# Pacing 313 gathers by an event each, with at most two gathers in flight

## The chip, the core and the metric

The kernel runs on one core of a Trainium2 chip, which has a matrix engine (TensorE, PE in the profile), a vector engine (VectorE, DVE), a scalar engine (ScalarE, ACT), GpSimd (POOL) and a queue engine (SyncE, SP), each with an instruction stream of its own. The streams meet in semaphores only. The metric is the device time of one launch in microseconds; lower is better.

## The reference

The function scores 2048 samples of 26 categorical fields. Each field of a sample picks one row of a table with 12500 rows; a row holds 16 embedding numbers and one first-order weight.

```
emb  = embed_table[f, x_idx]                       # (N, 26, 16)
lin1 = w1_table[f, x_idx].sum(1) + w1_bias
fm   = 0.5 * ((emb.sum(1) ** 2).sum(-1) - (emb * emb).sum((1, 2)))
mlp  = relu(relu(emb.reshape(N, 416) @ W1 + b1) @ W2 + b2) @ W3 + b3
last = x0 = emb.transpose(0, 2, 1)
for W in (cin_w0, cin_w1, cin_w2):                 # CIN layers
    last = einsum('ndl,ndf,klf->ndk', last, x0, W); feats.append(last)
out  = lin1 + fm + mlp + concat(feats).sum(1) @ lin_w + lin_b
```

## The kernel before

The CIN sum over its output channels lets the weights be folded into small matrices first; that is the setup, on PE, DVE and ACT, with its weights loaded by SP's and ACT's DMA queues. The samples then come in T = 16 tiles of 128. In each tile the embeddings lie in `emb` (three buffers, tile t in buffer t % 3), 128 partitions by 26 fields by 17 numbers.

*Where the rows come from.* POOL issues one indirect DMA, a gather, for each field of a tile (line 500): 128 rows of 68 bytes, one a partition. Tiles 0 and 1 gather all 26 fields. From tile 2 on the last four fields are not gathered: PE and DVE look them up in tables that are held in SBUF (`look_rows`, `keys_to_one_hot`, `pick_row`). So there are 2 * 26 + 14 * 22 = 360 gathers, numbered 0 to 359 below; gather 52 is the first of tile 2. Every gather adds 16 to its tile's semaphore `gathered[t]` when it has landed.

*What a tile does.* Its work is cut into 14 units: two halves in which the transposed embeddings are made (`x_high`, `x_low`), and NU = 12 units of the pairwise products (`square` on ACT, `z_low` on DVE, `main` and `picked` on PE). ACT ends its part of a unit by raising `hi_ready`, DVE by raising `lo_ready`, so both count units, 14 a tile; `x_no(t, h)` and `s_no(t, u)` give the number of a unit. PE, DVE and ACT pass units to one another through a ring of three PSUM banks.

*Who waits for the gathers.* ACT's `copy_by_position(t)` (lines 564 to 569) reorders tile t's embeddings into `by_pos`. It runs at unit u = 10 of tile t-1, waits for all of tile t's gathers and for its four looked-up fields, and stands in ACT's stream ahead of `square(t-1, 10)`. For the last tile the copy is cut in two (`copy_last_early`, `copy_last_late`) after u = 11. PE's `x_half` waits for the copy. In the setup the first copy, `copy_by_position(0)` at line 674, stands in ACT's stream ahead of six DMAs that move blocks of the setup (lines 676 to 682).

*What paces POOL* (lines 484 to 502). Before the gathers with the positions 16, 22, 34, 41 and 47 POOL waits for an event of the setup. Tile t >= 3 needs its buffer free: `by_pos_ready` and `row_sums` of tile t-3. From tile 2 on every second gather also waits for a unit of tile t-3 in `hi_ready`. Any number of gathers may be in flight.

Of the kernel before, what the change touches and what calls it, by code (L numbers as in the profile page):

```python
# [32 lines left out]
LOOKS = 4  # L33
FIRST_LOOK = 2
LATER = 2
EARLY = 18
PER_UNIT = 2
COLS = 98
WIDE = 26
SHARES = 4  # L40
# [57 lines left out]
def deepfm_cin_kernel(nc, x_idx, rows, w1_bias, mlp_w1, mlp_b1, mlp_w2, mlp_b2, mlp_w3, mlp_b3,  # L98
                      cin_w0, cin_w1, cin_w2, lin_w, lin_b, out):
    N, F = x_idx.shape  # L100
# [5 lines left out]
    T = N // P  # L106
# [13 lines left out]
    NC = 3  # L120
# [4 lines left out]
    NX = 2  # L125
    NPROD = NX + NU
# [14 lines left out]
    with ExitStack() as ctx:  # L141
# [6 lines left out]
        def sem(name):  # L148
            return ctx.enter_context(nc.semaphore(name))
# [19 lines left out]
        EMB = 3  # L169
# [132 lines left out]
        m_done, m_copied, b_done, b_copied = sem("m_done"), sem("m_copied"), sem("b_done"), sem("b_copied")  # L302
        ap_ready, bp_ready = sem("ap_ready"), sem("bp_ready")
        t_copied = sem("t_copied")
        y_blocks, yl_block, s_blocks = sem("y_blocks"), sem("yl_block"), sem("s_blocks")
        y_copied, y_stored = sem("y_copied"), [sem(f"y_stored{n}") for n in range(7)]
        moved_in, t_in = [sem(f"moved_in{g}") for g in range(3)], sem("t_in")
        t_step, total_ready = sem("t_step"), sem("total_ready")
        by_row_done, by_row_copied = sem("by_row_done"), sem("by_row_copied")
        za_done, zlin_done = sem("za_done"), sem("zlin_done")  # L310
# [10 lines left out]
        keys_first_in, keys_in = sem("keys_first_in"), [sem(f"keys_in{b}") for b in range(2)]  # L321
        one_hot_ready, rows_out = sem("one_hot_ready"), sem("rows_out")
        look_masked, looked = sem("look_masked"), sem("looked")
        gathered = [sem(f"gathered{t}") for t in range(T)]
        gathered_late = sem("gathered_late")
        by_pos_ready = sem("by_pos_ready")
        filled = sem("filled")
        hi_ready = sem("hi_ready")
        lo_ready = sem("lo_ready")
# [18 lines left out]
        def s_no(t, u):  # L348
            return NPROD * t + NX + u

        def looks(t):

            return LOOKS if FIRST_LOOK <= t < T else 0

        def look_no(t, i):
            return LOOKS * (t - FIRST_LOOK) + i

        def look_at(t, slot):

            n = LOOKS * t + slot - LATER  # L360
            return (FIRST_LOOK + n // LOOKS, n % LOOKS) if 0 <= n < look_no(T, 0) else None

        def looked_by(t):

            return min(max(LOOKS * t + 1 - LATER, 0), look_no(T, 0))
# [117 lines left out]
        @block.gpsimd  # L483
        def _(pool):
            pool.iota(row_base[:], pattern=[[V, F]], base=0, channel_multiplier=0).then_inc(base_ready, 1)
            SETUP_STEPS = {16: (m_done, 1), 22: (b_done, 1), 34: (s_blocks, 1), 41: (by_row_done, 1), 47: (za_done, 1)}
            for t in range(T):
                if t < 2:
                    pool.wait_ge(ix_ready, t + 1)
                if t >= EMB:  # L490
                    pool.wait_ge(by_pos_ready, 2 * (t - EMB + 1))
                    pool.wait_ge(row_sums, t - EMB + 1)
                for f in range(F - looks(t)):
                    if F * t + f in SETUP_STEPS:
                        signal, value = SETUP_STEPS[F * t + f]
                        pool.wait_ge(signal, value)
                    if t >= EMB - 1 and f and f % PER_UNIT == 0:
                        behind = s_no(t - EMB, NC + f // PER_UNIT - 1) if t >= EMB else s_no(0, f // PER_UNIT)
                        pool.wait_ge(hi_ready, behind + 1)
                    pool.indirect_dma_start(emb[t % EMB][:, f, :], None, rows,  # L500
                                            bass.IndirectOffsetOnAxis(row_ix[:, t, f:f + 1], 0)
                                            ).then_inc(gathered[t] if t < T - 1 or f < EARLY else gathered_late, 16)

        def within(mat, g, width):

# [14 lines left out]
        def _(act):  # L520
# [29 lines left out]
                               accum_out=first[:, t:t + 1]).then_inc(row_sums, 1)  # L550

            def copy_last_early():
                act.wait_ge(gathered[T - 1], 16 * EARLY)
                act.wait_ge(looked, look_no(T - 1, LOOKS))
                for fs in (slice(0, EARLY), slice(F - LOOKS, F)):
                    act.activation(by_pos[:, :, fs], emb[(T - 1) % EMB][:, fs, 0:D].rearrange("p f d -> p d f"), ACT.Copy)

            def copy_last_late():
                fs = slice(EARLY, F - LOOKS)
                act.wait_ge(gathered_late, 16 * (F - LOOKS - EARLY))  # L560
                act.activation(by_pos[:, :, fs], emb[(T - 1) % EMB][:, fs, 0:D].rearrange("p f d -> p d f"),
                               ACT.Copy).then_inc(by_pos_ready, 2)

            def copy_by_position(t):
                act.wait_ge(gathered[t], 16 * (F - looks(t)))
                if looks(t):
                    act.wait_ge(looked, look_no(t, LOOKS))
                act.activation(by_pos[:], emb[t % EMB][:, :, 0:D].rearrange("p f d -> p d f"),
                               ACT.Copy).then_inc(by_pos_ready, 2)
# [54 lines left out]
            def tile(t):  # L624
                for u in range(NC, NU):
                    if u == NU - 2 and t + 1 < T - 1:
                        copy_by_position(t + 1)
                    square(t, u)
                    if u == NU - 1 and t + 1 == T - 1:
                        copy_last_early()  # L630
                        copy_last_late()
                    if t == 0 and u in LOOK_SPLIT:
                        look_high(LOOK_SPLIT[u])
                    if t == 0 and u == 8:
                        second_high()
                    if u == 5:
                        hidden1(t)
                    if u == 7:
                        hidden1_high(t)
# [32 lines left out]
            act.wait_ge(keys_out, 1)  # L672
            act.activation(key_t[:], ps_s[0][0:T * LOOKS, 0:P], ACT.Copy).then_inc(keys_copied, 1)
            copy_by_position(0)
            act.wait_ge(moved_zeroed, 1)
            move(act, 3)
# [629 lines left out]
```

## Time and profile before

| | us |
|---|---|
| time, median of 3 runs | 512.74 (511.46 to 513.53) |
| profiled execution, first to last instruction | 694.2 |
| PE busy | 510.3 |
| DVE busy | 412.8 |
| ACT busy | 389.0 |
| POOL busy | 356.6 |
| mean granted TensorE clock | 0.863 |

The profiled execution is a different one from the timed runs. Its span is the only time that it has; of what lies around the span nothing is recorded. The page gives busy time by engine, the chain of work that ended last, and groups of like instructions with their mean and with the idle time before them. The windows view gives the same for chosen stretches.

### The profile page before, as it was taken

The page shows a single profiled execution, that of the slowest core. Times are in us where ns is not written, and L with a number is a line of the kernel's source. Part 1 is how long each engine was busy: PE and PEld are TensorE (multiplying, and loading weights), DVE is VectorE, ACT ScalarE, POOL GpSimd, SP SyncE. Part 2 cuts the span into 40 slices and gives each one's busy share as a digit, 9 for nine tenths or more (in the row PEclk, how much of TensorE's full clock was granted, in tenths as well). Part 3 has the DMA queues.
Part 4 walks back from the last instruction along what each step waited for, and adds up shares of the span by engine and source line. Part 5 has one row for each costly group of instructions (what it writes and reads, how often), then busy time and mean ns, then how long its engine had stood idle before and what let it go on. Part 6 is the DMA issues. An engine that isn't in the chain of part 4 may idle for free.

```text
span 694.2 us, 6825 instructions
## 1 busy us (share of the span) xinstructions
PE 510.3 (74%) x2235; PEld 415.1 (60%) x2235; DVE 412.8 (59%) x680; ACT 389.0 (56%) x759; POOL 356.6 (51%) x365
## 2 busy tenths in 40 slices
PE   2897918824696959588695959596886949599988
PEld 2865705723484838476574747475765737478666
DVE  6431227903475748376584847484765848478866
ACT  0321628604464847376574847484665748378875
POOL 6665666774465464637466454547374664510000
PEclk9995666975896979979798989899797979899999
DMA  8836434221111111202111111112021111100000
GB/s 176 163 21 117 88 62 103 7 7 5 5 6 7 4 6 4 7 4 8 5 6 5 5 6 6 6 4 8 3 9 5 6 5 5 6 3 1 0 1 0
DMA packets 21508, 15.57 MB, mean 22 GB/s; under 512 B 12790, under 2 KB 19811, under 8 KB 21347
## 3 DMA queue, kind: packets, MB, share of 16 engines
q0 software_dynamic: 11520, 3.16, 13.5%
q1 hardware_dynamic: 6949, 9.99, 5.9%
q10 hardware_dynamic: 3005, 2.01, 1.4%
q8 instruction: 18, 0.29, 0.2%
q14 instruction: 16, 0.12, 0.1%
HBM read 14.92 MB, written 0.21 MB: 22 GB/s over the span
## 4 chain that ended last, share of the span: by engine, by line
PE 28%; DVE 24%; another core or an unknown queue 18%; ACT 15%; issue 11%; DMA 3%; SPq 0%; DVEq 0%
DVE z_lo L803 5%; ACT ps_s L598 5%; ACT z_hi L591 4%; PE ps_y L1197 4%; PE ps_y L1198 3%; DVE ps_y L946 3%; DVE one_hot L935 3%; PE ps_s L1097 2%; DMA w_space<-cin_w 2%; DVE sums L829 2%; PE ps_q L1111 2%; ACT room_a L597 2%; DVE ps_q L814 2%; DVE emb L950 2%
## 5 line engine op out<-in xcount | busy, mean ns | idle before, releaser
L500 POOL DMA_INDIRECT emb<-rows,idx_raw x360 | 356.3, 990 | 253.7 <-issue 101.4
L803 DVE TENSOR_TENSOR z_lo<-ps_s,z_hi 128x512 fp32r<-128x512 f32 (+1 forms) x192 | 132.1, 688 | 138.9 <-ACT ps_s L598 87.6
L591 ACT ACTIVATE z_hi<-ps_s 128x512 fp32r<-128x512 f32 (+1 forms) x192 | 114.2, 595 | 171.9 <-remote 105.6
L1197 PE MATMUL ps_y<-look_hi,one_hot 128*128 128x442 f32 x224 | 92.6, 413 | 91.4 <-DVE one_hot L935 89.6
L598 ACT ACTIVATE ps_s<-ps_s 128x512 f32<-128x512 f32 (+1 forms) x192 | 113.5, 591 | 0.7
L1111 PE MATMUL ps_q<-z_lo,zw_hi 128*127 128x512 f32 (+1 forms) x192 | 86.9, 453 | 32.6 <-DVE z_lo L803 21.1
L1197 PEld LDWEIGHTS ps_y<-look_hi,one_hot 128*128 128x128 f32 x224 | 49.5, 221 | 101.0 <-DVE emb L950 57.1
L1198 PE MATMUL ps_y<-look_lo,one_hot 128*128 128x442 f32 x224 | 89.3, 400 | 0.0
L946 DVE SCALAR_TENSOR_TENSOR ps_y<-tables,look_place,ps_y 128x442 f32<-128x442 f32 x56 | 37.9, 677 | 78.6 <-remote 70.6
L1097 PE MATMUL ps_s<-xt,pick 128*128 128x512 f32 (+1 forms) x192 | 77.1, 414 | 8.6 <-ACT x L582 5.4
L1113 PE MATMUL ps_q<-z_hi,zw_hi 128*127 128x512 f32 (+1 forms) x192 | 78.9, 411 | 0.0
L1112 PE MATMUL ps_q<-z_hi,zw_lo 128*127 128x512 f32 (+1 forms) x192 | 78.9, 411 | 0.0
L1111 PEld LDWEIGHTS ps_q<-z_lo,zw_hi 128*127 128x127 f32 (+1 forms) x192 | 38.2, 199 | 54.9 <-issue 34.4
L1198 PEld LDWEIGHTS ps_y<-look_lo,one_hot 128*128 128x128 f32 x224 | 50.1, 224 | 4.6
L1097 PEld LDWEIGHTS ps_s<-xt,pick 128*128 128x128 f32 (+1 forms) x192 | 37.4, 195 | 18.9 <-issue 5.8
L574 ACT ACTIVATE xt<-ps_s 52x512 fp32r<-52x512 f32 x32 | 18.7, 592 | 45.4 <-remote 17.1
L1113 PEld LDWEIGHTS ps_q<-z_hi,zw_hi 128*127 128x127 f32 (+1 forms) x192 | 38.0, 198 | 9.4
L597 ACT ACTIVATE room_a<-ps_s 128x512 f32<-128x512 f32 x63 | 37.4, 593 | 5.9 <-DVE sums L814 5.9
L1112 PEld LDWEIGHTS ps_q<-z_hi,zw_lo 128*127 128x127 f32 (+1 forms) x192 | 38.5, 200 | 2.6
L593 ACT ACTIVATE z_hi<-ps_s 26x512 fp32r<-26x512 f32 x64 | 37.9, 592 | 0.8
L935 DVE TENSOR_TENSOR one_hot<-w_space,tables 128x512 fp32r<-128x512 f16 x52 | 36.1, 694 | 0.0
L950 DVE TENSOR_REDUCE emb<-ps_y 128x17 f32<-128x442 f32 x56 | 34.7, 619 | 1.9
(191 smaller groups left out, 765.0 us busy)
## 6 DMA issues: line engine op xcount, KB each, us to landing
emb<-rows,idx_raw POOLq DMA_INDIRECT x360
w_space<-rows SPq DMA_DIRECT2D x2, 728.9 KB
m_space<-rows SPq DMA_DIRECT2D x2, 728.9 KB
w_space<-key_scratch SPq DMA_DIRECT2D x1, 1408.0 KB
w<-cin_w SPq DMA_DIRECT2D x2, 416.0 KB, 4.8
w<-cin_w ACTq DMA_DIRECT2D x2, 416.0 KB, 7.6
w_space<-cin_w SPq DMA_DIRECT2D x2, 416.0 KB
w_space<-cin_w ACTq DMA_DIRECT2D x2, 416.0 KB
```

Source lines behind the costliest of these rows:

```text
L500: pool.indirect_dma_start(emb[t % EMB][:, f, :], None, rows, bass.IndirectOffsetOnAxis(row_ix[:, t, f:f + 1], 0)).then_inc(gathered[t] if ...
L591: act.activation(z_hi[0:k, c, :], ps[0:k, :], ACT.Square)
L598: act.activation(ps[0:k, :], ps[0:k, :], ACT.Square).then_inc(hi_ready, 1)
L803: z = dve.tensor_tensor(z_lo[0:k, u % NC, :], ps, z_hi[0:k, u % NC, :].bitcast(F32), ALU.subtract)
L935: dve.tensor_tensor(one_hot[n % 2][:], keys.to_broadcast([P, SHARES, P]), share_row.unsqueeze(2).to_broadcast([P, SHARES, P]), ALU.is_equa ...
L946: dve.scalar_tensor_tensor(by_place, place.unsqueeze(2).to_broadcast([P, WIDE, R]), look_place[:, t, i:i + 1], by_place, ALU.is_equal, ALU ...
L1097: pe.matmul(ps[0:CK[c], :], pick[:, e, c * P:c * P + CK[c]], xt[t % 2][:, 4 * h:4 * h + 4, :], start=True, stop=True).then_inc(filled, 1)
L1111: pe.matmul(ps, hi_w, lo_x, start=(c == 0), stop=False)
L1112: pe.matmul(ps, lo_w, hi_x, start=False, stop=False)
L1113: mm = pe.matmul(ps, hi_w, hi_x, start=False, stop=(c == NC - 1))
L1197: pe.matmul(o, one_hot[n % 2][:, j, :], look_hi[i][:, ws], start=(j == 0), stop=False)
L1198: mm = pe.matmul(o, one_hot[n % 2][:, j, :], look_lo[i][:, ws], start=False, stop=(j == SHARES - 1))
```

## The change

Each gather is given a number n. In the setup, gathers 16, 22, 28, 34 and 41 wait for an event (before: 16, 22, 34, 41, 47). From number 47 on, every gather waits for a half unit of its own: half step 4 + (n - 47) * 28 // 22, which is a count of `hi_ready` when even and of `lo_ready` when odd. From gather 2 on, each gather also waits until gather n - 2 has landed. Landings are counted in four semaphores that take turns, in place of one for each tile; a copy by position waits for all four.

```diff
--- before.py
+++ after.py
@@ -34,7 +34,9 @@
 FIRST_LOOK = 2
 LATER = 2
 EARLY = 18
-PER_UNIT = 2
+SETUP_GATHERS = 47
+LANDINGS = 4
+IN_FLIGHT = 2
 COLS = 98
 WIDE = 26
 SHARES = 4
@@ -321,8 +323,7 @@
         keys_first_in, keys_in = sem("keys_first_in"), [sem(f"keys_in{b}") for b in range(2)]
         one_hot_ready, rows_out = sem("one_hot_ready"), sem("rows_out")
         look_masked, looked = sem("look_masked"), sem("looked")
-        gathered = [sem(f"gathered{t}") for t in range(T)]
-        gathered_late = sem("gathered_late")
+        landed = [sem(f"landed{i}") for i in range(LANDINGS)]
         by_pos_ready = sem("by_pos_ready")
         filled = sem("filled")
         hi_ready = sem("hi_ready")
@@ -354,6 +355,19 @@
 
         def look_no(t, i):
             return LOOKS * (t - FIRST_LOOK) + i
+
+        def gather_no(t, f):
+
+            return sum(F - looks(s) for s in range(t)) + f
+
+        def wait_landed(eng, n):
+
+            eng.wait_ge(landed[n % LANDINGS], 16 * (n // LANDINGS + 1))
+
+        def wait_landed_all(eng, n):
+
+            for i in range(LANDINGS):
+                wait_landed(eng, n - i)
 
         def look_at(t, slot):
 
@@ -483,7 +497,17 @@
         @block.gpsimd
         def _(pool):
             pool.iota(row_base[:], pattern=[[V, F]], base=0, channel_multiplier=0).then_inc(base_ready, 1)
-            SETUP_STEPS = {16: (m_done, 1), 22: (b_done, 1), 34: (s_blocks, 1), 41: (by_row_done, 1), 47: (za_done, 1)}
+            SETUP_STEPS = {16: (m_done, 1), 22: (b_done, 1), 28: (s_blocks, 1), 34: (total_ready, 1), 41: (by_row_done, 1)}
+
+            def wait_for_pace(n):
+                if n in SETUP_STEPS:
+                    signal, value = SETUP_STEPS[n]
+                    pool.wait_ge(signal, value)
+                elif n >= SETUP_GATHERS:
+                    half = 2 * NX + (n - SETUP_GATHERS) * 2 * NPROD // (F - LOOKS)
+                    pool.wait_ge(lo_ready if half % 2 else hi_ready, half // 2 + 1)
+
+            n = 0
             for t in range(T):
                 if t < 2:
                     pool.wait_ge(ix_ready, t + 1)
@@ -491,15 +515,13 @@
                     pool.wait_ge(by_pos_ready, 2 * (t - EMB + 1))
                     pool.wait_ge(row_sums, t - EMB + 1)
                 for f in range(F - looks(t)):
-                    if F * t + f in SETUP_STEPS:
-                        signal, value = SETUP_STEPS[F * t + f]
-                        pool.wait_ge(signal, value)
-                    if t >= EMB - 1 and f and f % PER_UNIT == 0:
-                        behind = s_no(t - EMB, NC + f // PER_UNIT - 1) if t >= EMB else s_no(0, f // PER_UNIT)
-                        pool.wait_ge(hi_ready, behind + 1)
+                    wait_for_pace(n)
+                    if n >= IN_FLIGHT:
+                        wait_landed(pool, n - IN_FLIGHT)
                     pool.indirect_dma_start(emb[t % EMB][:, f, :], None, rows,
                                             bass.IndirectOffsetOnAxis(row_ix[:, t, f:f + 1], 0)
-                                            ).then_inc(gathered[t] if t < T - 1 or f < EARLY else gathered_late, 16)
+                                            ).then_inc(landed[n % LANDINGS], 16)
+                    n += 1
 
         def within(mat, g, width):
 
@@ -550,19 +572,19 @@
                                accum_out=first[:, t:t + 1]).then_inc(row_sums, 1)
 
             def copy_last_early():
-                act.wait_ge(gathered[T - 1], 16 * EARLY)
+                wait_landed_all(act, gather_no(T - 1, EARLY) - 1)
                 act.wait_ge(looked, look_no(T - 1, LOOKS))
                 for fs in (slice(0, EARLY), slice(F - LOOKS, F)):
                     act.activation(by_pos[:, :, fs], emb[(T - 1) % EMB][:, fs, 0:D].rearrange("p f d -> p d f"), ACT.Copy)
 
             def copy_last_late():
                 fs = slice(EARLY, F - LOOKS)
-                act.wait_ge(gathered_late, 16 * (F - LOOKS - EARLY))
+                wait_landed_all(act, gather_no(T - 1, F - LOOKS) - 1)
                 act.activation(by_pos[:, :, fs], emb[(T - 1) % EMB][:, fs, 0:D].rearrange("p f d -> p d f"),
                                ACT.Copy).then_inc(by_pos_ready, 2)
 
             def copy_by_position(t):
-                act.wait_ge(gathered[t], 16 * (F - looks(t)))
+                wait_landed_all(act, gather_no(t, F - looks(t)) - 1)
                 if looks(t):
                     act.wait_ge(looked, look_no(t, LOOKS))
                 act.activation(by_pos[:], emb[t % EMB][:, :, 0:D].rearrange("p f d -> p d f"),
```

## Rows read from the trace of the kernel before

**Rows 1.** The page: span, busy time, the costliest group (busy, mean ns | idle before).

```profile
span 694.2 us, 6825 instructions
...
PE 510.3 (74%) x2235; PEld 415.1 (60%) x2235; DVE 412.8 (59%) x680; ACT 389.0 (56%) x759; POOL 356.6 (51%) x365
...
L500 POOL DMA_INDIRECT emb<-rows,idx_raw x360 | 356.3, 990 | 253.7 <-issue 101.4
```

**Rows 2.** Windows: one tile with 23 gathers, one with 5.

```profile
core 0: us, PE busy (x) PEld busy (x) DVE busy (x) ACT busy (x) POOL busy (x), PEclk, DMA share, GB/s
452.40:490.50 38.10, 28.49 (x129) 22.97 (x129) 24.48 (x40) 23.11 (x45) 21.24 (x23) 0.90 0.16 5
605.20:634.00 28.80, 27.07 (x127) 22.23 (x127) 24.02 (x40) 22.91 (x45) 4.54 (x5) 0.97 0.06 3
```

**Rows 3.** Waits of the tile at 452.4 to 490.5: total us, times, longest.

```profile
PE ps_y L1197 <- DVE one_hot L935: 7.0, 2, 6.1
ACT z_hi L591 <- remote: 6.9, 1, 6.9
...
DVE ps_y L946 <- remote: 5.5, 1, 5.5
```

**Rows 4.** Timeline of POOL: gathers 46 to 48, and the last two.

```profile
start us, us, engine line op out<-in xcount [idle before <-releaser]
...
77.59 0.95 POOL L500 DMA_INDIRECT emb<-rows,idx_raw  x1 [0.30 <-issue]
78.84 0.94 POOL L500 DMA_INDIRECT emb<-rows,idx_raw  x1 [0.30 <-issue]
80.09 0.94 POOL L500 DMA_INDIRECT emb<-rows,idx_raw  x1 [0.30 <-issue]
...
608.76 0.95 POOL L500 DMA_INDIRECT emb<-rows,idx_raw  x1 [0.31 <-issue]
610.02 0.95 POOL L500 DMA_INDIRECT emb<-rows,idx_raw  x1 [0.30 <-issue]
```

**Rows 5.** Timeline of ACT: the last copies by position.

```profile
660.57 0.94 ACT L556 ACTIVATE by_pos<-emb 128x288 f32<-128x288 f32 x2
661.41 0.30 ACT L561 ACTIVATE by_pos<-emb 128x64 f32<-128x64 f32 x1
```

**Rows 6.** Windows after the last gather of tile 7, which started at 303.00.

```profile
303.00:303.90 0.90, 0.90 (x6) 0.72 (x5) 0.00 (x0) 0.29 (x1) 0.90 (x1) 1.00 0.25 7
...
305.20:305.50 0.30, 0.30 (x3) 0.30 (x3) 0.28 (x1) 0.28 (x1) 0.00 (x0) 1.00 0.14 7
305.50:305.80 0.30, 0.30 (x4) 0.30 (x3) 0.30 (x1) 0.30 (x1) 0.00 (x0) 1.00 0.04 4
305.80:306.40 0.60, 0.60 (x5) 0.51 (x4) 0.60 (x2) 0.05 (x2) 0.00 (x0) 1.00 0.00 0
```

**Rows 7.** Timeline: two releases of a gather by ACT.

```profile
271.05 0.19 ACT L549 ACTIVATION_READ_ACCUMULATOR first_all<-emb 128x1 f32 x1
...
272.00 0.94 POOL L500 DMA_INDIRECT emb<-rows,idx_raw  x1 [6.44 <-ACT first_all L549]
...
295.51 0.59 ACT L598 ACTIVATE ps_s<-ps_s 128x512 f32<-128x512 f32 x1
...
296.37 1.32 POOL L500 DMA_INDIRECT emb<-rows,idx_raw  x1 [4.18 <-ACT ps_s L598]
```

**Rows 8.** DMA packets, of 0 to 11.9 us and of 11.9 to 29.2 us.

```profile
q0 software_dynamic: 160, 0.04, 3.4%
...
q0 software_dynamic: 352, 0.10, 9.1%
```

**Rows 9.** Timeline of ACT in the setup: first copy by position and the moves.

```profile
48.97 0.94 ACT L568 ACTIVATE by_pos<-emb 128x416 f32<-128x416 f32 x1
49.37 0.47 ACTq L395 DMA_DIRECT2D w<-y_scratch  x1
50.50 3.07 ACTq L402 DMA_DIRECT2D w<-yl_scratch  x4
```

## The prediction

> **What bounds the kernel now.** I read the page first, then the windows by tile, then the waits, then POOL's own timeline and the DMA packets. The page: span 694.2 us, no engine above 74%, and POOL with 360 gathers of 990 ns [rows 1]. The profiled span is 181.5 us above the median of 512.74, so I asked what the profile stretches. The windows by tile answer: one tile with 23 gathers in it took 38.1 us, the one with 5 took 28.8, while DVE and ACT did the same work in both (24.5 and 24.0, 23.1 and 22.9 us) [rows 2]. The 9.3 us between them are waits of ACT and DVE for an event put down to "remote" (6.9 and 5.5 us), and of PE behind them [rows 3]. 15 tiles times 9.3 are 140 of the 181.5 us, so the plain runs have almost none of it. I don't use 694.2 as a base, therefore; I build the time from POOL's chain and from the tail, and hold the same construction against the median.
>
> POOL's chain: a gather's row is 0.95 us with 0.30 of issue after it, 1.25 from start to start [rows 4]. 22 a tile are 27.5 us. Gather 47 started at 78.84 [rows 4]; 312 steps of 1.25 later (390.0) the last of the 360 would start at 468.8; it lands 2.8 us later (below), and from ACT's last copy at 661.41 to the end of the span there are 32.8 us [rows 5]. 78.8 + 390.0 + 2.8 + 32.8 = 504.4, only 8 us under the median. So in the plain runs POOL issues gathers nearly without pause, and it is as close to the bound as the compute chain is: (512.7 - 32.8 - 78.8) / 15 = 26.7 us a tile, 1.9 a unit (14 units a tile, the two x halves counted), which is my estimate of the present pace. Whatever makes a gather step longer than 1.21 us (26.7 / 22) for good shows in the time.
>
> **The change, part by part.** *Removed*: the wait for hi_ready at every second gather, and the gate at gather 47. In plain runs POOL is late for them, so they end nothing; 0 us.
>
> *Pace*: gather n waits for half step 4 + (n - 47) * 28 // 22, each step 1.9 / 2 us: 1.27 half steps a gather, 1.21 us. Field 21 of tile t is let go at unit 18 counted from the start of tile t-2, and ACT's copy by position needs it at unit 26, the tenth u of tile t-1 being 12 units in. The lead is 7.5 units or 14.3 us; before it was more than a tile: the last gather of tile 15 started at 610.02, and the copy that waits for it at 660.57 [rows 4, 5]. By itself the pace costs nothing as long as POOL keeps 1.21 us; the cover is this lead.
>
> *The cap of two in flight*: gather n now also waits for the landing of n-2. Everything queued behind that wait on POOL is the next gathers; behind them waits ACT's copy, behind this ACT's squares, then DVE and PE. The price is half the round trip from a gather's start to the start that its landing permits. Landing: the last gather of a tile started at 303.00, the DMA engines were still 4% busy in 305.50 to 305.80 and idle after it [rows 6]: 2.8 us. Release: ACT's square ended at 296.10 and the gather that waited for this one semaphore started at 296.37, 0.27 later; a gather that stood behind two waits (by_pos_ready and row_sums) started 0.76 after the second came true (271.24 to 272.00) [rows 7]. So the round trip is 2.8 + 0.27 = 3.07 from below and 2.8 + 0.76 = 3.56 from above, a step of 1.53 or 1.78 us. The lower bound of any step is 1.25, POOL's own. Which of the two releases holds depends on whether POOL's sequencer has the next gather decoded while it waits. Gathers whose waits were true followed at 0.30 [rows 4], so it does run ahead; I take 1.53 and keep 1.78 for the range. Nothing excludes a landing shorter than 2.8 in a plain run, since the profile's semaphores are late in places; nothing shows one either.
>
> The Trainium skill's "DMA: Bandwidth & Descriptors", section "Anatomy of one DMA — SWDGE (gpsimd) path", has a fixed cost of about 2.0 us for such a DMA, setup and completion together. By it the round trip would be about 2.3 us, under the 2.5 of two steps of 1.25, and the cap would never bind.
>
> *Setup*: two are in flight from the first gather on. Five gathers were served by 11.9 us (160 packets at 32 each) and eleven more by 29.2 (352) [rows 8], with five or six in flight: 1.57 us each, some 8.6 in the ring for one. With two in flight a step under that load is between 1.53 and (8.6 + 0.27) / 2 = 4.4 us; I take 2.4, nearer the lower end, because most of the 8.6 was spent behind gathers of its own kind. Gathers 0 and 1 land at about 11.9, gathers 2 to 9 then take 8 * 2.4 = 19.2 (to 31), and 10 to 46 take 37 * 1.53 = 56.6: gather 47 starts at 87.7 instead of 78.84, between 81 and 92 for the two ends. Gather 25 lands at 31.1 + 15 * 1.53 + 2.8 = 56.9; ACT made the copy that needs it at 48.97 with the moves of the setup behind it [rows 9], so the setup is held up by 8 us as well, beside the same delay of POOL and not on top of it. The earlier gates (28, 34, 41) are passed by then; 0 us.
>
> *The four waits before each copy* in place of one: sequencer work on ACT while its own engine computes, 16 times; 0 us, and some 0.1 us each if ACT stood idle.
>
> **Sum**: 87.7 + 312 * 1.53 (477.4) + 2.8 + 32.8 = 600.7, say 601 us. POOL loses 1.53 - 1.21 = 0.32 us a gather on the pace, so the lead of 14.3 less 2.8 is spent after 36 gathers, and from the third tile on every tile is 22 * 1.53 = 33.7 us. The 8 us that the construction lacked for the kernel before are not added: they would be the compute chain's, and POOL is alone on the path now. With 1.78 the sum is 679, and 690 with the later end of the setup; with a landing 0.3 us shorter (step 1.385) it is 555.
>
> **Rivals.**
> - *The cap is idle.* In plain runs a gather is back in less than 2.5 us. For it: the whole profiled run is stretched. Against it: the 2.8 is told by DMA packets, not by semaphores, and PE's rows of the tile without gathers (28.8) are hardly stretched. Then only the setup's hold-up of 8 us is left: 521 us. The page cited above would give this case.
> - *Nothing shows.* As before, and the setup's delay is made up because the moves of the setup have slack: 511 to 515.
> - *Faster.* The mechanism: the waits for PE's late events stand only in tiles with gathers in them [rows 2, 3]. If 1 us a tile of this is real in plain runs, a gather stream that is spread over the units and never more than two deep removes it: 15 us off, 498. It decides only where the round trip is under 2.5 us, otherwise POOL's step swallows it. The median speaks against more than that: a tile is 26.7 us with DVE busy for 24.5.
> - *The change doesn't do what it says*: as POOL falls behind, each pace event is long past when its gather comes, and the spreading never takes place; only the cap acts. That is what my sum has.
>
> **How the numbers follow.** About 0.5% is what a measurement of this kernel can tell from no change. Cap binding with a step of 1.38 or more: 0.64, own range 555 to 690. Cap binding a little (525 to 555): 0.06. Cap idle with the setup's cost: 0.09. Nothing: 0.08. Faster: 0.13. So faster 0.13, same 0.08, slower 0.79. The range leaves out the extreme ends of both sides: 508 to 685.
>
> **What would show it.** Right: gathers from the 47th on start 1.5 us or more apart on average, alternating; POOL's idle time goes to the landings; tiles of 33 us or more, all alike; ACT's copy by position waits for gathers; PE's clock falls in the gaps. Wrong: starts 1.25 us apart with idle time put down to hi_ready or lo_ready, that is the pace; then the cap is idle. The setup step is right if the first square comes some 8 us later. The forecast fails if the round trip of a gather in a plain run is under 2.5 us.

## The result, and the profile after

| | before | after |
|---|---|---|
| time, median | 512.10 us (510.35 to 513.53, 4 runs) | 757.09 us (755.99 to 758.51, 4 runs) |
| ratio, 95% interval | | 1.4809 (1.4768 to 1.4849) |

The runs of before are those taken beside the kernel after; they agree with the 512.74 of the table ahead. The kernel is 245 us slower, and 156 us slower than forecast. The direction and the mechanism, the cap of two, were forecast; the size was not, and 757 lies well above the end of the range (685).

First the page of the kernel after: its span, busy times, share of the chain that ended last, two of its groups, and the DMA issue row of the gathers, whose last number is the median from issue to landing.

```profile
span 753.9 us, 7174 instructions
...
PE 498.7 (66%) x2235; PEld 413.1 (55%) x2235; DVE 411.4 (55%) x680; ACT 387.5 (51%) x759; POOL 346.6 (46%) x365
...
DMA 45%; PE 19%; ACT 14%; issue 12%; DVE 8%; POOL 1%; POOLq 0%; ACTq 0%; DVEq 0%
...
L521 POOL DMA_INDIRECT emb<-rows,idx_raw x360 | 346.2, 962 | 373.7 <-DMA emb<-rows,idx_raw 242.5
...
L590 ACT ACTIVATE by_pos<-emb 128x416 f32<-128x416 f32 x15 | 14.2, 947 | 223.2 <-DMA emb<-rows,idx_raw 223.2
...
emb<-rows,idx_raw POOLq DMA_INDIRECT x360, 3.0
```

Beside [rows 1], every engine's busy time is what it was or less. What is new is idle time: POOL stands idle for 373.7 us before its gathers (253.7 before, the largest part of it put down to "issue", time in which no awaited event shows), and the releaser is now a landing. 45% of the chain that ended last is DMA, nearly all of it the flight of gathers. ACT's copy by position, for which the trace of before has no idle time, waits for gathers all 15 times, 223.2 us in total. This profiled execution took 755.99 us, 2.1 more than its span, so here span and time go together.

The windows of two tiles, cut at ACT's copies, answer to [rows 2]:

```profile
298.76:341.02 42.26, 27.77 (x128) 23.26 (x128) 24.34 (x40) 22.97 (x45) 20.75 (x22) 0.82 0.15 6
341.02:384.24 43.22, 28.77 (x128) 23.96 (x128) 24.33 (x40) 22.97 (x46) 21.75 (x22) 0.82 0.14 5
```

DVE (24.3 us) and ACT (23.0) do the same work as before in tiles that last 42 to 43 us. The granted clock of PE is 0.82 in them. The waits of the first of the two windows (engine, line, what it waited for; us in total, times, longest) show how the loss is passed on, from a landing to ACT's copy, and from that to PE and DVE:

```profile
DVE z_lo L825 <- ACT ps_s L620: 16.8, 8, 13.2
POOL emb L521 <- DMA emb<-rows,idx_raw: 14.2, 9, 2.0
ACT by_pos L590 <- DMA emb<-rows,idx_raw: 13.8, 1, 13.8
PEld ps_s L1107 <- issue: 13.2, 1, 13.2
PE ps_s L1107 <- ACT by_pos L590: 12.8, 1, 12.8
```

Next POOL's timeline in the middle of the run, which answers to [rows 4].

```profile
401.59 0.94 POOL L521 DMA_INDIRECT emb<-rows,idx_raw  x1 [0.73 <-DVE z_lo L825]
403.65 0.94 POOL L521 DMA_INDIRECT emb<-rows,idx_raw  x1 [1.11 <-DMA emb<-rows,idx_raw]
405.35 0.94 POOL L521 DMA_INDIRECT emb<-rows,idx_raw  x1 [0.76 <-DMA emb<-rows,idx_raw]
407.43 1.04 POOL L521 DMA_INDIRECT emb<-rows,idx_raw  x1 [1.14 <-DMA emb<-rows,idx_raw]
```

From each gather to the next but one it is 3.76 and 3.78 us (401.59 to 405.35, 403.65 to 407.43). The releasers "ACT ps_s" and "DVE z_lo" that also stand in such rows are other raises of the pace's semaphores. The value that a gather waits for had been reached 14 us or more before it started, for every gather from the 47th on, and the landing is what ended the wait. The semaphore instructions, which the timeline leaves out, say why the round trip is so long (start, end, instruction):

```
403.65 404.59 DMA_INDIRECT
404.61 404.62 EVENT_SEMAPHORE    L365, waits for the landing of the gather that started at 401.59
405.35 406.29 DMA_INDIRECT       carries the wait for the pace
```

In these traces a gather carries one wait itself, the one that the kernel states first. A second wait is an instruction of its own ahead of it. The kernel after states the pace first, so the landing is the separate one. The landing came 3.0 us after its gather's start (401.59 to 404.61), and the next gather started 0.74 us after it. Landing and release, the time from a landing to the start that it permits, make a round trip of 3.0 + 0.74 = 3.74 us, against the forecast's 3.07.

Last the setup, which answers to [rows 4, 8]. The gathers 26 to 32, and 47; ahead of them the page's row of what the DMA engines moved (GB/s, 40 slices of 18.8 us):

```profile
GB/s 190 119 21 51 84 192 8 5 5 6 5 5 5 5 5 6 5 6 5 6 5 5 5 6 4 5 5 5 6 4 6 5 6 5 6 4 5 5 2 0
```

```profile
63.23 0.94 POOL L521 DMA_INDIRECT emb<-rows,idx_raw  x1 [1.54 <-DMA emb<-rows,idx_raw]
64.47 0.94 POOL L521 DMA_INDIRECT emb<-rows,idx_raw  x1 [0.30 <-issue]
67.16 0.94 POOL L521 DMA_INDIRECT emb<-rows,idx_raw  x1 [1.74 <-DMA emb<-rows,idx_raw]
68.40 0.94 POOL L521 DMA_INDIRECT emb<-rows,idx_raw  x1 [0.30 <-issue]
70.38 0.94 POOL L521 DMA_INDIRECT emb<-rows,idx_raw  x1 [1.03 <-DMA emb<-rows,idx_raw]
71.62 0.94 POOL L521 DMA_INDIRECT emb<-rows,idx_raw  x1 [0.31 <-DMA emb<-rows,idx_raw]
78.46 0.94 POOL L521 DMA_INDIRECT emb<-rows,idx_raw  x1 [5.89 <-DMA emb<-rows,idx_raw]
...
115.85 0.94 POOL L521 DMA_INDIRECT emb<-rows,idx_raw  x1 [2.54 <-DMA emb<-rows,idx_raw]
```

The gather at 70.38 (number 30) was away for 7.8 us. The setup has two bursts of loads, one to 38 us and one that peaks between 94 and 113 (192 GB/s), and the gather lies where the second begins. With two in flight POOL stood still for that (5.89). The row at 115.85 is gather 47, which had started at 78.84 [rows 4].

The whole span then adds up from three pieces: 115.85 to gather 47, 312 steps of 1.936 to the last gather at 720.0, and 33.9 to the end.

### The profile page after: what moved, and what is told of

It reads as the page before. It is cut to its first block, busy times and chain, and to the rows that moved or that the text cites. A ratio compares the mean times of both kernels' runs of the same rounds, so it can differ in the third digit from the quotient of the medians.

```text
span 753.9 us, 7174 instructions
## 1 busy us (share of the span) xinstructions
PE 498.7 (66%) x2235; PEld 413.1 (55%) x2235; DVE 411.4 (55%) x680; ACT 387.5 (51%) x759; POOL 346.6 (46%) x365
## 4 chain that ended last, share of the span: by engine, by line
DMA 45%; PE 19%; ACT 14%; issue 12%; DVE 8%; POOL 1%; POOLq 0%; ACTq 0%; DVEq 0%
DMA emb<-rows,idx_raw 44%; ACT ps_s L620 4%; ACT z_hi L613 4%; PE ps_y L1219 3%; PE ps_s L1107 3%; PE ps_y L1220 3%; DVE z_lo L825 2%; ACT by_pos L590 2%; ACT z_hi L615 1%; POOL emb L521 1%; PE ps_q L1133 1%; PE ps_q L1134 1%; PE ps_q L1135 1%; PE ps_s L1119 1%; PE ps_mlp L1204 1%
## 5 line engine op out<-in xcount | busy, mean ns | idle before, releaser
L521 POOL DMA_INDIRECT emb<-rows,idx_raw x360 | 346.2, 962 | 373.7 <-DMA emb<-rows,idx_raw 242.5
L1107 PE MATMUL ps_s<-tables,by_pos 128*52 128x128 f32 x128 | 29.9, 386 | 217.0 <-ACT by_pos L590 209.4
L1107 PEld LDWEIGHTS ps_s<-tables,by_pos 128*52 128x52 f32 x128 | 17.3, 146 | 227.0 <-issue 223.2
L590 ACT ACTIVATE by_pos<-emb 128x416 f32<-128x416 f32 x15 | 14.2, 947 | 223.2 <-DMA emb<-rows,idx_raw 223.2
L1133 PE MATMUL ps_q<-z_lo,zw_hi 128*127 128x512 f32 (+1 forms) x192 | 83.3, 434 | 6.1 <-DVE z_lo L825 5.7
L1134 PE MATMUL ps_q<-z_hi,zw_lo 128*127 128x512 f32 (+1 forms) x192 | 76.8, 400 | 0.0
L1135 PE MATMUL ps_q<-z_hi,zw_hi 128*127 128x512 f32 (+1 forms) x192 | 76.4, 398 | 0.0
L1119 PE MATMUL ps_s<-xt,pick 128*128 128x512 f32 (+1 forms) x192 | 74.5, 402 | 1.8 <-DVE z_lo L825 1.6
```

The lines of the kernel that those rows point to most:

```text
L521: pool.indirect_dma_start(emb[t % EMB][:, f, :], None, rows, bass.IndirectOffsetOnAxis(row_ix[:, t, f:f + 1], 0)).then_inc(landed[n % LAND ...
L1107: mm = pe.transpose(ps[0:XR, c * P:(c + 1) * P], by_pos[:, d:d + 2, :].rearrange("p d f -> p (d f)"), ident)
L1119: pe.matmul(ps[0:CK[c], :], pick[:, e, c * P:c * P + CK[c]], xt[t % 2][:, 4 * h:4 * h + 4, :], start=True, stop=True).then_inc(filled, 1)
L1133: pe.matmul(ps, hi_w, lo_x, start=(c == 0), stop=False)
L1134: pe.matmul(ps, lo_w, hi_x, start=False, stop=False)
L1135: mm = pe.matmul(ps, hi_w, hi_x, start=False, stop=(c == NC - 1))
```

## The experiments

The theory that the runs were to test: only the cap costs; its step, the time from one gather's start to the next, is (landing + release) / depth, where the depth is the number of gathers that may be in flight; and the release is long because the landing is the second wait. Against it stood, among others that the expectations name, that the wait for a unit's event costs something itself, and that the landings are slower than a trace tells. Each run below came with runs of the kernel before on the same chip (medians 511.4 to 512.1). "Last gather" is the start of gather 359.

### Three in flight

```diff
-IN_FLIGHT = 2
+IN_FLIGHT = 3
```

> Cap of three in flight instead of two, nothing else. Theory A (the time is POOL's step, and the step is the round trip of a gather, 3.0 us to the landing plus 0.74 from the landing to the next start, divided by the number in flight): the step falls from 1.94 to 1.25 to 1.30 us, the setup's gather 47 starts at about 95 us instead of 116, and the time is 95 + 312 * 1.28 + 37 = 530 us (520 to 545). Theory B (waiting for two semaphores before every gather costs POOL's sequencer its time whatever the depth): the step stays above 1.6 us and the time above 640. Theory C (the pace is what holds): no change, 757.

Measured: 557.4 us (554.5 to 557.7), 1.087 (1.083 to 1.091). Its gathers (busy, mean ns; idle before them):

```profile
L521 POOL DMA_INDIRECT emb<-rows,idx_raw x360 | 353.5, 982 | 162.4 <-issue 89.8
```

One gather more in flight gives back 200 of 245 us, so the cap is the cause. The miss by 27 us was mine: gather 47 started at 89.6, and the step was 1.366 us where (3.0 + 0.74) / 3 = 1.25 would have hidden behind POOL's own 1.25. Over the 312 steps this is 26 us more than in the kernel without waits in the tiles (below). The trace puts 5 of them in the first 13 gathers, where landings take up to 7.7 us, 7.7 at three gathers that start late with nothing awaited (last section), and 9 behind gathers that landed too late for the third one after them; the other 4 are spread.

### The landing stated first

```diff
-                    wait_for_pace(n)
                     if n >= IN_FLIGHT:
                         wait_landed(pool, n - IN_FLIGHT)
+                    wait_for_pace(n)
```

> The two waits of a gather change places: the wait for the landing is stated first, that for the pace second. Nothing is taken away. Theory A, refined (of two waits the first stated rides on the gather itself, which then starts 0.27 us after it, and the second stands in an instruction of its own, after which the gather starts only 0.74 us later): the round trip falls from 3.77 to 3.30 us, the step from 1.94 to about 1.69, and the time by 312 * 0.24 = 75 us, to 680 (670 to 690). Rival (the order of two waits doesn't matter, the 0.74 is the price of any wait for a DMA): 757 as before.

Measured: 676.4 us (674.9 to 680.6), 1.319 (1.315 to 1.323); step 1.708. The two lines swapped are worth 81 us. POOL's gathers by the releases that ended their idle time (us, times):

```profile
L521 POOL DMA_INDIRECT emb<-rows,idx_raw x360: 938/946/2277, 3.8 to 645.5; - x180
...
  DMA emb<-rows,idx_raw: 255.2, 291
```

The landing rides on the gather now, and the pace wait is the separate one, long since true. Measured from the landing's semaphore to the start, the release falls from 0.76 us to 0.26 (medians; gather 45, for one, landed at 112.48 and gather 47 started at 112.74). By the mean landing of 3.06 us the step would be 1.66; the measured one is 0.05 longer.

### The pace alone

```diff
+                    elif n >= SETUP_GATHERS:
+                        half = 2 * NX + (n - SETUP_GATHERS) * 2 * NPROD // (F - LOOKS)
+                        pool.wait_ge(lo_ready if half % 2 else hi_ready, half // 2 + 1)
```

This goes into the kernel before, in place of its wait at every second gather, together with the new places of the setup's waits; no cap.

> The kernel before with the new pace (a half unit for each gather from the 47th on, the new setup gates) and without any cap. Theory A: the pace costs nothing, its lead of half a tile covers POOL's 1.25 us a gather: 510 to 518 us. Rival 1 (the later start of each tile's gathers makes the copies late, because POOL's 27.5 us a tile are longer than the 26.7 of the others): 520 to 540. Rival 2 (spreading the gathers relieves the other engines): under 505.

Measured: 514.3 us (512.7 to 517.5), 1.0059 (1.0033 to 1.0086). Of the 245 us the pace and the new setup waits have 2.5 together (1.7 to 4.4 by the interval).

### The cap alone

The kernel after without the three lines shown above: from gather 47 on the landing is the only wait.

> The changed kernel without its pace from gather 47 on: only the cap of two and the free buffer are waited for, so a gather has one wait, for the landing of n - 2. Theory A: the step is (3.0 + 0.27) / 2 = 1.64 plus some 0.05 of other delays, as with the waits swapped, and the time 670 to 690 us; that it is equal to the run with the waits swapped says that the pace itself costs nothing beside the cap. Rival (the pace holds part of the time): clearly below the run with the waits swapped, under 660.

Measured: 679.6 us (677.8 to 680.3), 1.326 (1.322 to 1.330); step 1.694. That is the kernel with the landing first but for 3 us (the last gather starts 1.5 us earlier here), though it has no pace. So beside the cap the pace costs nothing as an event; in the kernel after it costs 77 us by its mere place ahead of the landing.

### Three in flight and the landing first

Both edits above together.

> Cap of three and the wait for the landing stated first. Theory A: the round trip of 3.27 us over three is 1.09 us, under POOL's own 1.25 to 1.29, so the cap no longer acts once the setup is over; what is left of the 557 of the run with three is the setup's hold-up (gather 47 at about 88 us where the pace alone has 74.5): 514 + 13 = 527 us (522 to 533). Rival (the 557 came from the depth of three itself, not from the order of waits): 550 or more.

Measured: 540.7 us (539.6 to 541.2), 1.055 (1.052 to 1.059); step 1.337, gather 47 at 83.2. The order is worth 17 us here, 81 with two in flight. I expected 527 because I took a step of 1.28 to be hidden; it is not (below).

### The setup without the cap

```diff
-                    if n >= IN_FLIGHT:
-                        wait_landed(pool, n - IN_FLIGHT)
+                    m = n - 2 * F
+                    if m >= IN_FLIGHT:
+                        wait_landed(pool, m - IN_FLIGHT)
```

The landings of tiles 0 and 1 are counted by a semaphore for each tile, as before the change.

> The changed kernel, but gathers 0 to 53 (the setup's and the first two of tile 2) are not capped; the copies of tiles 0 and 1 wait for counters of their own. Theory A (POOL's chain sets the end from gather 47 on): the step stays 1.94, gather 47 starts at about 75 instead of 115.9, and the time falls by these 41 us and by some 3 for the few steps freed: 713 us (708 to 720). Rival (the setup's delay is hidden under the first tiles): 745 or more.

Measured: 719.2 us (713.0 to 719.9), 1.401 (1.393 to 1.410). Gather 47 starts at 73.4 and the step is 1.954. So the cap in the setup costs 38 of the 245 us, about what gather 47 is late by (37.0 us, or 42 beside this run).

### One in flight

```diff
-IN_FLIGHT = 2
+IN_FLIGHT = 1
```

> Cap of one in flight. Theory A: the step is the whole round trip, 3.0 + 0.74 + 0.05 = 3.79 us; gather 47 starts near 185 us (47 steps of 3.3 and the load of the setup), and the time is 185 + 312 * 3.79 + 37 = 1404 us (1370 to 1440). Rival (what costs is a fixed amount for each wait, not the round trip): less than twice 1.94 by far, under 1000.

Measured, in one run: 1422.9 us. With one in flight the round trip can be read directly, as the distance of two starts:

```profile
701.80 0.94 POOL L521 DMA_INDIRECT emb<-rows,idx_raw  x1 [2.84 <-DMA emb<-rows,idx_raw]
705.62 0.94 POOL L521 DMA_INDIRECT emb<-rows,idx_raw  x1 [2.88 <-DMA emb<-rows,idx_raw]
709.38 0.94 POOL L521 DMA_INDIRECT emb<-rows,idx_raw  x1 [2.81 <-DMA emb<-rows,idx_raw]
```

3.76 to 3.82 us, 3.83 on average over all 312 steps. The separate waits before the last two ended at 704.90 and 708.65, 3.1 and 3.0 us after the start that they waited for and 0.72 and 0.73 before the next start. The step at depths of 1, 2 and 3 is 3.83, 1.94 and 1.37 us: 3.83 divided by the depth gives 1.92 and 1.28.

### The kernel before without its waits in the tiles

```diff
-                    if t >= EMB - 1 and f and f % PER_UNIT == 0:
-                        behind = s_no(t - EMB, NC + f // PER_UNIT - 1) if t >= EMB else s_no(0, f // PER_UNIT)
-                        pool.wait_ge(hi_ready, behind + 1)
```

> The kernel before without its wait for hi_ready at every second gather; the buffer's waits and the setup's gates stay. My step that the old pace ends nothing in plain runs: 512 us (509 to 515). Rival (the old pace protects something, gathers that run ahead disturb the others): 518 or more. Of the profiled span, 694 us before and 515 with the new pace alone: if the stretch comes from gathers that run more than a tile ahead, it stays above 650 here; if it comes from the bursts between old pace events, it is gone.

Measured: 511.6 us (510.4 to 514.6), 0.9994 (0.997 to 1.002). The wait that the change removes ended nothing. This is nearly the kernel before, and its profiled execution is a plain one (span 510.2, granted clock 0.997). So it shows what [rows 1 to 3] could not. From its page: the chain that ended last, and the gathers; then a window of one tile.

```profile
POOL 60%; issue 20%; PE 7%; ACT 5%; DMA 4%; DVE 3%; SPq 0%; POOLq 0%; DVEq 0%
...
L497 POOL DMA_INDIRECT emb<-rows,idx_raw x360 | 353.7, 983 | 117.9 <-issue 108.8
```

```profile
309.03:336.41 27.38, 26.30 (x130) 22.05 (x129) 24.15 (x40) 22.85 (x46) 20.75 (x22) 1.00 0.21 7
```

From gather 23 on POOL issues gathers without a pause, and its own stream, with the issue time between the gathers, is 80% of the chain. It needs 28.0 us a tile (gathers 96 to 338; the mean step of 1.283 from gather 47 on has some longer gathers of the first tile in it), the compute chain 27.4. POOL is the slower of the two, and lives on the lead that it has from the setup. By lead I mean the time from the start of a tile's last gather to the copy that needs it. It is 9.1 us for tile 1, falls by some 0.6 a tile, and ends at 3.1, the landing itself, where the copy has to wait.

### The pace seven units earlier

The pace alone lost 0.5%. I took the cause to be its smaller lead over the copy.

```diff
-                        half = 2 * NX + (n - SETUP_GATHERS) * 2 * NPROD // (F - LOOKS)
+                        half = max(2 * NX + (n - SETUP_GATHERS) * 2 * NPROD // (F - LOOKS) - NPROD, 2 * NX)
```

> The new pace alone, but each event half a tile earlier (14 half units, 7 units), so the lead of a gather over its copy is 14.5 units instead of 7.5. Theory: the 2.4 us of the pace alone are its lead used up, because POOL needs 1.28 us a gather where the units allow 27.4 / 22 = 1.245 (312 * 0.035 = 11 us lost against a lead of about 14 less the landing of 3). With seven units (13.7 us) more the copies don't wait: 512 us, as without a pace (ratio to before 0.998 to 1.002). Rival (the 2.4 us are the price of a second kind of event, or of the new setup gates): 514 again.

Measured: 514.0 us (512.7 to 517.4), 1.0054 (1.0032 to 1.0075). Nothing came back, so it is not the lead of the pace.

### Three in flight, the landing first, the setup free

> Cap of three, landing stated first, and the first 55 gathers not capped (54 of them as in the run with the uncapped setup). The run with the capped setup had 540.7: its gather 47 started at 83.2 instead of 74.5, and after it POOL had no lead left and its 1.29 to 1.34 us a gather stood in the path. Theory: with the setup free, the round trip of 3.27 / 3 = 1.09 us hides under POOL's own step, and the time is that of the pace alone, 514 us (512 to 520). Rival (a cap of three costs in the loop by itself): 530 or more.

Measured: 521.6 us (520.1 to 522.1), 1.018 (1.015 to 1.022). The last gather starts at 482.6, 10.9 us later than in the kernel without waits in the tiles (471.7), and the time is 10.0 longer: 2.0 us at gather 47 (73.3 for 71.4), 8.9 from 312 steps of 1.312 in place of 1.283. Of these, 4 fall between gathers 47 and 60, where gathers 52 to 54 took 6.7 to 7.6 us to land. I had let the first tiles' lead absorb both delays. With POOL the slower chain it absorbs neither.

### Two waits that are long since true

```diff
+                    if t >= 2:
+                        pool.wait_ge(ix_ready, 2)
+                        pool.wait_ge(idx_in, 16)
```

This stands before each gather from tile 2 on, in the kernel without its waits in the tiles.

> The kernel without pace and cap, with two waits added before each gather from tile 2 on, both for events of the first microseconds that are long true; so each gather has an instruction of its own for the second wait ahead of it. Theory (the 0.74 us are paid only when the second wait is what the gather really waits for, because POOL's sequencer otherwise has them done while the gather before runs): 512 us, step 1.28. Rival (each second wait costs POOL's sequencer its 0.4 to 0.7 us in any case): a step of 1.6 or more and over 600 us.

Measured: 511.8 us (510.3 to 513.4), 1.0005 (0.9988 to 1.0022); step 1.285. The separate wait stands in the trace, and the gather behind it still follows 0.30 after the one before. So a separate wait that is already true costs nothing; the 0.74 us is paid when the separate wait is what the gather really waits for.

### The new places of the setup's waits alone

The 2.5 us of the pace were still open; what the two kernels with the pace had in common beside it were the setup's waits. This run is the kernel without its waits in the tiles, with this edit:

```diff
-            SETUP_STEPS = {16: (m_done, 1), 22: (b_done, 1), 34: (s_blocks, 1), 41: (by_row_done, 1), 47: (za_done, 1)}
+            SETUP_STEPS = {16: (m_done, 1), 22: (b_done, 1), 28: (s_blocks, 1), 34: (total_ready, 1), 41: (by_row_done, 1)}
```

> The kernel before without its wait at every second gather, and with the new gates of the setup (28 and 34 in place of 34 and 47). Two theories for the 0.5% that the two kernels with the pace alone lost. If it is the gates: 514 us, a ratio of 1.004 to 1.006, and a copy by position that waits 0.5 to 2 us for gathers in most tiles from 280 us on, as in them. If it is the pace events: 512 us, a ratio of 0.998 to 1.002, and the copies wait in the last tiles alone.

Measured: 514.1 us (513.2 to 515.6), 1.0055 (1.0034 to 1.0075), the same as both kernels with the pace. The timeline of POOL at the gathers 27 to 29:

```profile
44.58 0.95 POOL L497 DMA_INDIRECT emb<-rows,idx_raw  x1 [0.30 <-issue]
48.44 0.94 POOL L497 DMA_INDIRECT emb<-rows,idx_raw  x1 [2.91 <-PE ps_t L1067]
49.68 0.94 POOL L497 DMA_INDIRECT emb<-rows,idx_raw  x1 [0.30 <-issue]
```

So the 0.5% belongs to the new places, not to the pace. Gather 28 now waits 2.91 us, 2.6 more than the 0.30 of a gather that waits for nothing. In the kernel with the old places, the wait for `s_blocks` stands at gather 34 and is true when POOL comes. The same gather waited 3.70 and 2.89 us in the two kernels with the pace.

What this takes away is lead. The last gather of tile 1 and the copy that needs it, first with the new places, then with the old:

```profile
78.01 0.95 POOL L497 DMA_INDIRECT emb<-rows,idx_raw  x1 [0.30 <-issue]
84.64 0.94 ACT L565 ACTIVATE by_pos<-emb 128x416 f32<-128x416 f32 x1
```

```profile
77.22 0.94 POOL L497 DMA_INDIRECT emb<-rows,idx_raw  x1 [0.31 <-issue]
86.34 0.94 ACT L565 ACTIVATE by_pos<-emb 128x416 f32<-128x416 f32 x1
```

The lead is 6.6 us for 9.1. So ACT's copies wait for gathers from 308 us on instead of 392. The copy at the same place in the new kernel and in the one with the old places:

```profile
308.49 0.95 ACT L565 ACTIVATE by_pos<-emb 128x416 f32<-128x416 f32 x1 [0.73 <-issue]
```

```profile
309.03 0.95 ACT L565 ACTIVATE by_pos<-emb 128x416 f32<-128x416 f32 x1
```

A lead that shrinks by 28.0 - 27.4 = 0.6 us a tile and is 2.5 us smaller should be spent some four tiles sooner; 392 - 308 = 84 us are three. The last gather starts at 474.3 against 471.7, 2.6 us later, but this is not the wait at gather 28 carried through: up to gather 184 POOL is only 0.7 late, and the rest comes after it, while the copies wait and the gathers themselves are a little longer (170.4 us for 168.4 in total over the next 175). In the kernel with the earlier pace POOL is not late at all at gather 47 and 1.8 us late at the end. Why the gathers are longer there is not shown, and a shift of 1 or 2 us in one traced execution is no more than the timed runs differ by.

## Why the prediction was wrong, point by point

**The cap binds from the setup on, POOL is alone on the path, every tile is equally long, the copy by position waits for gathers, and the pace costs nothing**: right. The rival in which the cap is idle would need a round trip under 2.5 us; even with the landing first it is 3.4 on average. The faster rival also needed that, and the pace without the cap was not faster either (1.0059).

**The release: the step that failed.** The prediction wrote "Gathers whose waits were true followed at 0.30 [rows 4], so it does run ahead; I take 1.53". Both halves are true and the conclusion is not. POOL does run ahead over waits that are true (two of them cost nothing), but that says nothing about a wait that is not. [Rows 7] had both cases, 0.27 for a gather behind one wait and 0.76 behind two, and the kernel after puts its gathers behind two, in the bad order. The value to take was the upper one; the row was at hand, with two waits ahead of the gather as here. Its size by itself is 312 * (0.76 - 0.27) / 2 = 76 us; the swap of the two lines measured 81. The lower value, 0.27, was right for a gather whose landing is the wait that it carries (0.26 in the kernel with the landing first).

**The landing.** I took 2.8 us, the last DMA packet; the semaphore is seen at 3.0. With this, with the gathers that are away longer (the mean is 3.04), and with three late starts that no landing explains (last section), the step is 1.936 where my upper end was 1.78: 312 * 0.16 = 49 us (unrounded 48.7).

**The setup.** Gather 47 at 87.7, no later than 92: it was 115.9, and this is 28 us. The first ten gathers came nearly as forecast (gather 9 at 32.9 for 31). What failed is "10 to 46 take 37 * 1.53". They took 1.70 on average from number 10 to 25, with the landing as their only wait nearly everywhere, and 2.50 from there to 47 ((115.9 - 60.7) / 22), beside the second burst of loads: gathers 30 and 31 were away 7.8 and 7.9 us, and four of those from 40 to 45 between 6.1 and 7.5. [Rows 8] priced the first burst, and the working had no term for a second. Its later end was also added up wrongly: eight steps of 4.4 us give 11.9 + 35.2 + 56.6 = 104, not 92, and the sum at that end is 695 us, not 690. The measured 116 and 757 lie beyond these too. The prediction's 8 us for ACT's first copy were 14.9 (63.82 for 48.97), beside POOL's delay as forecast.

**The tail**: 33.9 us in the span and about 3 outside it or between this run and the median, for 35.6; 1.5 us.

76 + 49 + 28 + 1.5 = 155, of the 156 missed; the rest is the rounding of 1.535 to 1.53.

**The new setup waits at 0 us.** "The earlier gates (28, 34, 41) are passed by then; 0 us" holds for the kernel after, where the cap has POOL late. Without the cap the new places cost 2.5 us of lead and about 0.5% of the time.

**[Rows 1]'s 694.2 us** were rightly not used as a base, and the construction on POOL's chain (504 for 512.7) was sound. The reading "as close to the bound as the compute chain is" was too weak: POOL is the slower chain of the kernel before, by 0.6 us a tile, if that kernel behaves as the one without waits in the tiles, which takes the same time. Why that profiled execution was stretched is not shown by any run; nor did another one repeat it.

**The page's rule.** The rival stood on the figure of the Trainium skill's "DMA: Bandwidth & Descriptors", section "Anatomy of one DMA — SWDGE (gpsimd) path". Its fixed cost of about 2.0 us is not the round trip: start to landing is 3.0 here. Counted from the end of POOL's 0.94 us it is 2.06, which agrees. The measurement decides: a gather is back after 3.0 us and not after 2.0.

The second wait as an instruction of its own is what the Trainium skill's "Perfetto Trace Analysis", section "Identifying Dependency Chains", describes: additional conditions may be put into event-semaphore instructions ahead of the instruction. The trace agrees, and adds a price of 0.74 us where such a condition comes last.

No version here beats the kernel before. The best of them, without the waits in the tiles, is the same within 0.3%.

## What to carry to other kernels

A cap on transfers in flight sets a step of (start to landing + release) / depth. Take the landing from the semaphore, not from the last packet, and check the step against the issuing engine's own. If it can't be hidden, raise the depth before anything else.

Where an instruction waits for two things, state first the one that will come last. The other order cost half a microsecond for each round trip here (0.76 for 0.26), and 81 us in all.

Before costing a wait at nothing because it is true when reached, ask which chain has no slack. Here the issuing engine had none: one wait moved to an earlier gather of the setup took 2.5 us of its lead, and the whole run was about 2.5 us longer.

## What was unexpected of the hardware

- A wait in an instruction of its own costs nothing when it is already true (step 1.285 with it, 1.283 without), and 0.72 to 0.76 us from its end to the gather's start when it is not. For the wait that the gather carries, the one stated first, it is 0.26 us from the landing to the start.
- The time to land depends on what else moves. It is 3.0 us in the tiles, between 2.9 and 3.9 where it shows in the kernel without waits in the tiles, and up to 8.7 in the setup of the kernel after, where at most two gathers were in flight. With one in flight it still reached 9.5 us there. So those delays are not a queue of gathers. That they come from the bulk loads is inferred from their times; no run took the loads away.
- Three in flight should suffice by the mean (3.8 / 3 = 1.27, or 3.3 / 3 = 1.11 with the landing first), yet the steps were 1.366 and 1.337 (1.312 with the setup free), not 1.283. A mean does not tell how deep a cap must be: a few long landings right behind the setup made up a fifth to nearly half of each excess.
- Three gathers, numbers 113, 223 and 333, start late in the kernel after although everything that they wait for is true: 3.4 us after the landing in place of 0.76. With one and with three in flight the same three do so; with the landing first, or without the pace, it is 1.8 us in place of 0.26. They are 110 gathers apart. The kernel without waits in the tiles shows no such gap. What causes it is not shown by any run. One of them in the kernel after:

```profile
240.95 0.94 POOL L521 DMA_INDIRECT emb<-rows,idx_raw  x1 [0.39 <-issue]
246.12 0.95 POOL L521 DMA_INDIRECT emb<-rows,idx_raw  x1 [4.22 <-issue]
247.37 0.94 POOL L521 DMA_INDIRECT emb<-rows,idx_raw  x1 [0.30 <-issue]
```

- Mean granted clock: 0.997 in the kernel without waits in the tiles, 0.869 with two in flight and the landing first, 0.830 in the kernel after, 0.676 with one in flight. In the two long tiles shown first its mean was 0.82, and PE's 128 matrix products took 27.77 us there for 26.30 at 1.00. As PE waited for ACT's copy, this cost nothing that can be seen beside the cap.
